# Gate projection and its scan ahead of the key projection, carry and exponentials ahead of the queries

## The reference

```python
xn = _layernorm(x)
q, k, v = xn @ Wq, xn @ Wk, xn @ Wv          # 16, 8, 8 heads of 128
log_g = log_sigmoid(6.906768 + xn @ Wg)      # one gate per token and k/v head
G = cumsum(log_g, over tokens)
a = (q k^T / sqrt(128))**2 * exp(G_t - G_s), causal
y = (a @ v) / (sum(a) + 1e-6)
s = y @ Wc + bc
h = silu((xn @ gate_w^T) * gate_s) * ((xn @ up_w^T) * up_s)
g = silu((h @ down_w^T) * down_s)
x = x + s * g
```

## Time and profile before

| what | us |
|---|---|
| median of 3 runs | 8217.06 |
| lowest and highest of them | 8092.64, 8550.13 |
| the profiled execution itself | 8090.58 |
| its span, first to last instruction, slowest core | 8088.8 |
| spans of the eight cores | 8060.1 to 8088.8 |
| mean granted TensorE clock of the cores | 0.917 to 0.920 |

### The profile page before, as it was taken

The page is one execution under the profiler, slowest core; times in us unless marked ns, Lnnn a source line. Parts: engine busy times, 40 slices in busy tenths (PEclk is TensorE's granted clock), DMA queues, the critical chain, the costliest instruction groups (busy, mean ns, idle before and its releaser), DMA issues.

```text
span 8088.8 us, 107937 instructions; the slowest of 8 cores (8060.1 to 8088.8 us)
## 1 busy us (share of the span) xinstructions
PE 6772.8 (84%) x43624; PEld 3403.5 (42%) x43624; DVE 994.6 (12%) x2180; ACT 2008.7 (25%) x2296; POOL 557.8 (7%) x1192
## 2 busy tenths in 40 slices
PE   7999977559999897666999988777689998977777
PEld 3444433324444344433444334554234443445553
DVE  1000002220000011122000001111200000111002
ACT  2211011212210004521121011665121200046661
POOL 0000001100000000100000000000000000000000
PEclk9999988779999898888999999888899998998998
DMA  4444442253444431034444443101534444310004
GB/s 95 75 77 71 68 75 43 42 135 74 78 74 70 76 68 32 22 92 103 77 78 73 68 84 57 25 17 35 134 75 78 77 70 78 66 45 22 22 12 125
DMA packets 240203, 544.23 MB, mean 67 GB/s; under 512 B 103841, under 2 KB 112161, under 8 KB 232033
## 3 DMA queue, kind: packets, MB, share of 16 engines
q0 software_dynamic: 93392, 377.58, 26.6%
q1 hardware_dynamic: 127890, 126.18, 5.4%
q10 hardware_dynamic: 18432, 33.56, 1.6%
HBM read 864.31 MB, written 50.33 MB: 113 GB/s over the span
## 4 chain that ended last, share of the span: by engine, by line
PE 63%; ACT 12%; DMA 10%; DVE 8%; issue 4%; POOL 2%; ACTq 1%; DVEq 0%; SPq 0%; POOLq 0%
PE pball L409 30%; PE pball L463 15%; ACT a2p L718 11%; PE pball L751 3%; PE pball L602 3%; PE pball L527 3%; PE pball L502 3%; DVE a2p L798 2%; PE pball L861 2%; DMA x<-x 2%; DMA out<-x 2%; DMA ar<-wk 2%; DMA ar<-wq 2%; POOL a2p L727 2%; PE pball L702 2%
## 5 line engine op out<-in xcount | busy, mean ns | idle before, releaser
L409 PE MATMUL pball<-ar 128*128 128x512 bf16 x11264 | 2441.9, 380 | 5.2 <-DVE ar L289 5.2
L409 PEld LDWEIGHTS pball<-ar 128*128 128x128 bf16 x11264 | 1104.1, 98 | 1341.5 <-issue 18.9
L718 ACT ACTIVATE a2p<-pball,sc_tok 128x1024 bf16<-128x1024 f32 (+3 forms) x1152 | 1203.9, 1045 | 881.3 <-PE pball L758 438.8
L463 PE MATMUL pball<-ar 128*128 128x512 bf16 x5632 | 1266.5, 386 | 89.7 <-DVE scrA L475 83.4
L751 PE MATMUL pball<-ar,a2p 128*128 128x128 bf16 x8448 | 916.1, 225 | 203.8 <-DVE ar L823 104.6
L751 PEld LDWEIGHTS pball<-ar,a2p 128*128 128x128 bf16 x8448 | 785.6, 104 | 400.4 <-issue 316.1
L702 PE MATMUL pball<-ar 128*128 128x512 bf16 x2304 | 745.4, 412 | 183.8 <-ACT a2p L718 177.9
L463 PEld LDWEIGHTS pball<-ar 128*128 128x128 bf16 x5632 | 556.4, 99 | 799.1 <-issue 163.7
L758 PE MATMUL pball<-ones_col,a2p 128*128 128x1 bf16 x8448 | 849.8, 172 | 0.0
L758 PEld LDWEIGHTS pball<-ones_col,a2p 128*128 128x128 bf16 x8448 | 737.0, 98 | 121.8 <-issue 35.7
L420 ACT ACTIVATE a2p<-pball,gsc_s 128x512 bf16<-128x512 f32 x352 | 242.6, 689 | 1864.8 <-PE pball L409 1838.0
(11 more groups left out here) (92 smaller groups left out, 2303.9 us busy)
## 6 DMA issues: line engine op xcount, KB each, us to landing
ar<-gw POOLq DMA_DIRECT2D x176, 512.0 KB, 5.1
ar<-uw POOLq DMA_DIRECT2D x176, 512.0 KB, 7.4
ar<-dw POOLq DMA_DIRECT2D x176, 512.0 KB, 5.1
ar<-wq POOLq DMA_DIRECT2D x64, 512.0 KB, 5.1
x<-x ACTq DMA_DIRECT2D x128, 256.0 KB, 3.5
ar<-wc POOLq DMA_DIRECT2D x16, 2048.0 KB, 15.8
out<-x SPq DMA_DIRECT2D x128, 256.0 KB, 3.1
x_buf<-x SPq DMA_DIRECT2D x16, 1024.0 KB, 6.0
```

The lines of the kernel that those rows point to most:

```text
L409: b.op("tensor", lambda e, half=half, cg=cg, ts=ts, bank=bank, slot=slot: e.matmul(pb[bank][:, 0:512], gu_sl(slot, half, cg), xnT_sl(cg, t ...
L463: b.op("tensor", lambda e, ic=ic, tc=tc, slot=slot: e.matmul(pb[tc][:, 0:512], hdn_sl(ic, tc * 128, 128), dn_sl(slot, ic % 4), start=(ic = ...
L718: b.op("scalar", lambda e, src=src, dst=dst, j=j, jh=jh: e.activation(dst, src, AF.Square, scale=sc_tok[:, j * 8 + jh:j * 8 + jh + 1]), ma ...
```

## The change

Three pieces of the list of operations change places, in each of the four blocks:

- The gate projection and the gate chain move from behind the values to ahead of the keys, directly behind the issue of the value weight. The matmuls use banks 6 and 7 in place of 0 and 1.
- The carry matmuls, the addition of the carry and the two exponentials move from behind the queries to ahead of them, directly behind the values. The eight rounds of transposes stay behind the queries.
- The value weight gets a semaphore of its own, `g_wv`, so that the wait of the gate matmuls for their weight (loaded once at the start) does not count the value weight.

No operation is added or left out. The core of the diff:

```diff
@@ -167,6 +167,7 @@
         s_g64 = b.sem("s_g64")
         s_bc = b.sem("s_bc")
         g_wr = b.sem("g_wr")
+        g_wv = b.sem("g_wv")
         g_wq = [b.sem(f"g_wq{i}") for i in range(2)]
         g_wc = [b.sem(f"g_wc{i}") for i in range(2)]
         g_gu = [b.sem(f"g_gu{i}") for i in range(2)]
@@ -484,8 +485,51 @@
                     b.op("gpsimd", lambda e: e.memset(zro[:, :], 0.0), mark=gm,
                          waits=[scr2_free[0]])
                     wv_st = ar1[:, 0:NCG * 1024].rearrange("p (c i) -> p c i", c=NCG)
-                    b.dma("gpsimd", g_wr, wv_st, wv_d, waits=[(tm, s3_done)])
-                    wv_rdy = (g_wr, g_wr.n)
+                    b.dma("gpsimd", g_wv, wv_st, wv_d, waits=[(tm, s3_done)])
+                    wv_rdy = (g_wv, g_wv.n)
+                    for ts in range(NSUB):
+                        for cg in range(NCG):
+                            w = []
+                            if cg == 0:
+                                w = [wrdy["wg"], (vm, xnT_half[ts]), bank_free[6 + ts]]
+                            b.op("tensor", lambda e, cg=cg, ts=ts: e.matmul(
+                                pb[6 + ts][0:8, 0:512], wgp[:, cg, :], xnT_sl(cg, ts * 512, 512),
+                                start=(cg == 0), stop=(cg == NCG - 1)),
+                                mark=tm, waits=w)
+                        b.op("vector", lambda e, ts=ts: e.tensor_copy(gscr, pb[6 + ts][0:8, 0:512]),
+                             mark=vm, waits=[(tm, tm.n), (sm, g_done), (s_g64, s_g64.n)])
+                        bank_free[6 + ts] = (vm, vm.n)
+                        b.dma("sync", s_g64, xbF[ts * 8:ts * 8 + 8, 0:512], gscr,
...
+                    b.op("scalar", lambda e, o=g_th: e.activation(o, xbF[0:NRG, 0:512],
+                                                                  AF.Tanh,
+                                                                  bias=cc("offh", NRG),
+                                                                  scale=cc("half", NRG)),
+                         mark=sm, waits=[(s_g64, s_g64.n), (vm, ln_marks[-1]), (gm, gm.n)])
...
+                    b.op("vector", lambda e, o=g_sg, i=g_cu: e.tensor_copy(o, i[:, 511:512]),
+                         mark=vm)
                     for kd in range(HK):
                         slot = kd % 2
...
-                    for ts in range(NSUB):
-                        for cg in range(NCG):
...
-                            b.op("tensor", lambda e, cg=cg, ts=ts: e.matmul(
-                                pb[ts][0:8, 0:512], wgp[:, cg, :], xnT_sl(cg, ts * 512, 512),
...
-                    for qd in range(HQ):
-                        slot = qd % 2
...
-                    s5_done = tm.n
                     b.op("tensor", lambda e, i=g_sg: e.matmul(
                         pb[2][0:NRG, 0:1], msgb[0:NRG, 0:NRG], i, start=True, stop=False),
                          mark=tm, waits=[(vm, vm.n), bank_free[2], (s_misc, s_misc.n),
...
                     ge_done = sm.n
+                    for qd in range(HQ):
+                        slot = qd % 2
...
+                    s5_done = tm.n
                     for jl in range(NTC2):
```

More of the change, by code:

```diff
@@ new lines, in emit_phase2 @@
+                    g_th = xbF[0:NRG, 512:1024]
+                    g_sp = xbF[0:NRG, 1024:1536]
+                    g_q = xbF[0:NRG, 1536:2048]
+                    g_cu = xbF[0:NRG, 512:1024]
+                    g_e2 = xbF[0:NRG, 1536:2048]
+                    g_e1 = xb16[0:NRG, 0:512]
+                    g_sg = xbF[0:NRG, 500:501]
+                    g_of = xbF[0:NRG, 501:502]
+                    b.op("scalar", lambda e, o=g_th: e.activation(o, xbF[0:NRG, 0:512],
[3 more added lines that the diff above has]
+                         mark=sm, waits=[(s_g64, s_g64.n), (vm, ln_marks[-1]), (gm, gm.n)])
@@ new lines, in emit_phase2 @@
+                    b.op("vector", lambda e, o=g_sp, i=g_th: e.tensor_scalar(
+                        o, i, -0.5, 0.5, ALU.mult, ALU.add),
+                         mark=vm, waits=[(sm, sm.n)])
+                    b.op("vector", lambda e, o=g_q, i=g_sp: e.tensor_scalar(
+                        o, i, 1.0 / 9.0, 1.0 / 8.0, ALU.mult, ALU.add), mark=vm)
+                    for k in range(7, 0, -1):
+                        b.op("vector", lambda e, o=g_q, i=g_sp: e.tensor_mul(o, o, i),
+                             mark=vm)
+                        b.op("vector", lambda e, k=k, o=g_q: e.tensor_scalar(
+                            o, o, 1.0 / k, None, ALU.add), mark=vm)
@@ L489, in emit_phase2 @@
+                    b.op("vector", lambda e, o=g_q, i=g_sp: e.tensor_mul(o, o, i), mark=vm)
+                    b.op("vector", lambda e, o=g_cu, i=g_q, z=zro: e.tensor_tensor_scan(
+                        o, i, z, 0.0, ALU.add, ALU.add),
+                         mark=vm, waits=[(gm, gm.n)])
+                    b.op("vector", lambda e, o=g_sg, i=g_cu: e.tensor_copy(o, i[:, 511:512]),
+                         mark=vm)
                     for kd in range(HK):
@@ L644, in emit_phase2 @@
                     ge_done = sm.n
+                    for qd in range(HQ):
+                        slot = qd % 2
+                        b.dma("gpsimd", g_wq[slot],
+                              ar3[:, slot * 2048:slot * 2048 + 2048]
+                              .rearrange("p (c i) -> p c i", c=NCG),
+                              wq_d[qd], waits=[wq_free[slot], dn_free[slot]])
+                        wslice = (g_wq[slot], g_wq[slot].n)
+                        qbase = 4 + (qd % 2) * 2
+                        for cg in range(NCG):
+                            for ts in range(NSUB):
+                                bank = qbase + ts
+                                w = []
+                                if cg == 0:
+                                    w = [wslice, bank_free[bank]]
+                                b.op("tensor", lambda e, qd=qd, cg=cg, ts=ts, bank=bank, slot=slot: e.matmul(
+                                    pb[bank][:, 0:512], wq_sl(slot, cg),
+                                    xnT_sl(cg, ts * 512, 512),
+                                    start=(cg == 0), stop=(cg == NCG - 1)),
+                                    mark=tm, waits=w)
+                        for ts in range(NSUB):
+                            bank = qbase + ts
+                            b.op("vector", lambda e, qd=qd, ts=ts, bank=bank: e.tensor_copy(
+                                qT_sl(qd, ts * 512, 512), pb[bank][:, 0:512]),
+                                mark=vm, waits=[(tm, tm.n), (tm, s3_done)])
+                            bank_free[bank] = (vm, vm.n)
+                            wq_free[slot] = (vm, vm.n)
+                    s5_done = tm.n
                     for jl in range(NTC2):
@@ L899, in emit_phase2 @@
                     b.wait("sync", s, s.n)
-                for s in g_wq + g_wc + g_gu + g_dn + [g_wr]:
+                for s in g_wq + g_wc + g_gu + g_dn + [g_wr, g_wv]:
                     b.wait("gpsimd", s, s.n)
```

11 lines of the change are left out of this document (1 added, 10 removed).

## The result

The changed kernel takes 8004.4 us (median of 10 runs) against a forecast of 7995 and a range of 7965 to 8120; the kernel before takes 8250.9 us (median of 10). The ratio is 0.9887 with a 95% interval of 0.9872 to 0.9901: 1.1% faster, and clear of no change. Eighteen readings of the kernel before lie between 8066 and 8082 us (median 8076), eighteen of the changed one between 7974 and 7985 (median 7980): 96 us less, where the forecast's sum said 95.9.

The account below looks back on a forecast made before the run. TensorE, busy 84% of the span, was taken as the bound, with time only in its gaps. Terms 28.0 - 1.6 + 50.0 + 19.5 = 95.9 us off 8090.6 gave 7995 us, range 7965 to 8120.

Parts of the forecast that it names:

- Gate matmuls hidden: After the down projection: gate matmuls fit inside the 30.5 us key-weight wait, taking 28.0 us off the path over four blocks.
- Stores, Tanh and chain: Behind the moved gate matmuls: two small SyncE stores, ScalarE's Tanh and the 12.6 us DVE chain cost nothing.
- Carry: Between values and queries: four small carry matmuls now on the path cost 0.4 us a block, 1.6 us lost.
- The stop at the third slice: In the queries: TensorE's wait for the third weight, held up by the gate chain on DVE, goes; 50.0 us saved.
- The head: From end of queries to attention: 9.8 us in place of 14.85, block 4 saving 4.5; 19.5 us in all.
- sign of a wrong step: At the end of the queries: attention starting more than 11 us after them would prove a step wrong.
- Rival 1: Before the keys: key weight late by up to the DVE chain's 12.6 us a block, total 8045 us; chance 0.08.
- Rival 2: After the queries: attention begins no earlier because key and value load or another wait ends last, 8014 us; chance 0.08.
- Rival 3: Before the keys: each of 18 DVE operations makes the weight transfer miss a portion, 8219 us, slower; chance 0.02.
- the step from the sum to whether it would be seen: Whole kernel: 1.2% gain held below the 2% a measurement can about tell; 0.95 on within 2%, 0.03 on faster.

## Why the prediction was right in its sum and wrong on whether it would show

- **Gate matmuls hidden.** Right. The first matmul of the keys did not move (+2.2 us in four blocks, within the spread of the cores), and the passage from values to queries lost 27.1 us for 26.4. The time of the matmuls, bounded at 13.7 us for the slow clock throughout, was 9.0, at a mean granted clock of 0.79.
- **Stores, Tanh and chain.** Right that they cost nothing; the unknown first store took 7.4 to 12.1 us (8.9 in the rows) and lay between my bounds. The run with the keys first showed that this was a matter of slack: with less of it the Tanh does hold up the keys.
- **Carry.** Taken at 0.4 us, bounded by 0.2 and 1.4; measured 0.28.
- **The stop at the third slice.** Right, 51.6 us for 50.0, and by the cause named: moving the chain alone brings it. Its two parts came out as well: idle time 43 us less for 42.0, and 8.5 us less busy time for the 8 credited to the restarts (mean of the eight cores).
- **The head.** 19.2 us for 19.5. In block 4 the value load ended last, as said, but later than I took it: attention began 10.2 to 11.7 us after the queries for 10.2. On four of the eight cores that is over the 11 us which I had named as a sign of a wrong step; the step is the landing of that load, taken from one block of one core, and it cost less than 1 us.
- **Rival 1** (key weight late by the chain) fell, though the changed kernel alone does not test it well: its chain starts at 2784.5, after the key weight has landed. The 24 operations set beside the transfer do, from 10.3 us after its issue on. **Rival 2** (no gain at the head) fell by the run with the carry put back. **Rival 3** (slower, missed portions) fell with rival 1.
- **What failed** is the step from the sum to whether it would be seen: "The gain is real in the account but below the 2% which a measurement of this kernel can about tell from no change", and with it the 0.95 on within 2%, as if that meant no change. By size the case is within 2%, but no row stood behind 2% as the limit of what can be told; the only spread reckoned with was that of the three runs, 8092.6 to 8550.1 around a median of 8217.1. What the runs showed in its place: a ratio with an interval of 0.9872 to 0.9901, which is clear of 1 and contains the 1.2% of the sum, and readings of one kernel within 11 to 16 us, 0.2% of the time and at most a sixth of the 96 us gained. The eight cores of before, 8060 to 8089, had shown a spread of that small kind. A sum of 96 us should have been stated as faster, by 1.2%. For the same reason the part of the range above 8045 was no outcome of the change: it was drawn out to 8120 for the distance of one execution to the median of three.

## What to carry to other kernels

Before pricing a long chain on a side engine, look at what stands behind it in that engine's queue: here 12.6 us of small DVE work cost TensorE 10 to 12 us at a weight transfer two steps away, and only its place mattered. A wait that serves as cover can be a mere order of requests, as here; once it is removed, the work hidden in it wants another place, here behind four key slices rather than ahead of them (7 us a block for 18). And where a forecast is a sum of measured waits, judge whether it will show by how closely like executions agree, here 0.2%, and not by the spread of all runs.

## What the runs showed that I had not expected

- A 16 KB store from SyncE that lands within 2.2 us behind the values in the kernel before took 7.4 to 12.1 us beside the 4 MB weight transfer, though that transfer's own traffic leaves half of the slices empty.
- The second move, worth 18 us behind the first, gains nothing alone.
- The eight rounds of 16-column transposes, set between full query slices, cost 0.27 us each on TensorE, more than the 0.18 us from start to start between the slices.
